# Local attention and retention: ScalarE normalises the shifted tile and squares the retention, the mask comes from row halves, VectorE rotates the last queries, the first release stands first

## The reference

```python
qk = jnp.einsum('bhsd,bhtd->bhst', qr, kr) * mask
denom = jnp.clip(jnp.abs(jax.lax.stop_gradient(qk).sum(-1, keepdims=True)), 1.0, None)
qk = qk / denom
out = jnp.einsum('bhst,bhtd->bhsd', qk, vr).transpose(0, 2, 1, 3)
mu = out.mean(-1, keepdims=True)
var = ((out - mu) ** 2).mean(-1, keepdims=True)
out = (out - mu) / jnp.sqrt(var + 1e-05)
out = jax.nn.silu(g) * out.reshape(B, S, H * head_dim)
return out @ Wo + bo
```

```python
h = shift_token(x)              # second half of the features comes from the token before
q, k, v = jnp.split(h @ wqkv, 3, axis=-1)
q = l2norm(q) * qs
k = l2norm(k) * ksc
q, k = rotary_xpos(q, k)
o = local_attention(q, k, v)    # mask = (i < j) | (i > j + WINDOW) | (j == -1)
x = x + o @ wo
h = shift_token(x)
mu = h.mean(-1, keepdims=True)
var = h.var(-1, keepdims=True)
h = (h - mu) / jnp.sqrt(var + 1e-05) * lg + lb
a, g = jnp.split(h @ w1 + b1, 2, axis=-1)
x = x + (a * jax.nn.gelu(g, approximate=False)) @ w2 + b2
```

## Time and profile before

| | us |
|---|---|
| median of three runs | 1041.69 |
| lowest, highest | 1039.55, 1044.32 |
| the profiled execution, its own time | 1053.3 |
| its span, first to last instruction | 1051.6 |
| TensorE busy | 879.2 (84%) |
| VectorE busy | 662.8 (63%) |
| ScalarE busy | 491.4 (47%) |
| GpSimd busy | 477.9 (45%) |

### The profile page before, as it was taken

The page is one execution under the profiler, slowest core; times in us unless marked ns, Lnnn a source line. Parts: engine busy times, 40 slices in busy tenths (PEclk is TensorE's granted clock), DMA queues, the critical chain, the costliest instruction groups (busy, mean ns, idle before and its releaser), DMA issues.

```text
span 1051.6 us, 19025 instructions
## 1 busy us (share of the span) xinstructions
PE 879.2 (84%) x6808; PEld 540.4 (51%) x6808; DVE 662.8 (63%) x1690; ACT 491.4 (47%) x1010; POOL 477.9 (45%) x501
## 2 busy tenths in 40 slices
PE   5876998889875788899987669988998587888998
PEld 2553676457643344444545536764676344444445
DVE  3897795569678655430168887946795776653302
ACT  2213775367634555542141147744775344655321
POOL 2666883188532422310056678823885324222101
PEclk9999999999996889899989999999999866998999
DMA  9100010011000000000000010100110000000000
GB/s 356 57 1 22 21 28 6 11 26 33 7 1 1 1 2 1 2 1 21 11 13 2 2 32 17 27 2 21 27 28 1 1 1 1 2 1 1 1 20 21
DMA packets 11636, 21.67 MB, mean 21 GB/s; under 512 B 1424, under 2 KB 6928, under 8 KB 11024
## 3 DMA queue, kind: packets, MB, share of 16 engines
q1 hardware_dynamic: 11248, 18.60, 6.0%
q10 hardware_dynamic: 288, 1.78, 0.4%
HBM read 11.87 MB, written 1.05 MB: 12 GB/s over the span
## 4 chain that ended last, share of the span: by engine, by line
PE 53%; DVE 28%; POOL 8%; issue 5%; ACT 4%; DMA 1%; SPq 0%; POOLq 0%; DVEq 0%; ACTq 0%
PE bank L831 11%; PE bank L384 9%; DVE arena L1212 4%; PE bank L742 4%; PE bank L639 3%; PE bank L821 3%; DVE arena L1060 3%; PE bank L709 2%; DVE arena L895 2%; PE bank L728 2%; POOL arena L1722 2%; POOL arena L1730 2%; DVE arena L953 2%; DVE arena L1071 2%; PE bank L414 2%
## 5 line engine op out<-in xcount | busy, mean ns | idle before, releaser
L384 PE MATMUL bank<-consts_sb,arena 128*128 128x128 f32 x1040 | 166.8, 304 | 98.7 <-DVE arena L903 24.3
L384 PEld LDWEIGHTS bank<-consts_sb,arena 128*128 128x128 f32 x1040 | 129.7, 155 | 165.8 <-issue 79.9
L1356 ACT ACTIVATE arena<-bank 128x512 f32<-128x512 f32 (+2 forms) x300 | 147.5, 556 | 143.2 <-PE bank L384 84.8
L1642 POOL TENSOR_TENSOR rstd<-vareps,neghalf 128x1 f32<-128x1 f32 x96 | 53.0, 553 | 250.2 <-DVE vareps L890 248.8
L1212 DVE TENSOR_REDUCE arena<-bank 128x2 f32<-128x1024 f32 (+3 forms) x128 | 98.0, 819 | 47.7 <-PE bank L696 47.0
L1722 POOL TENSOR_TENSOR arena<-arena,neghalf 128x16 f32<-128x16 f32 x32 | 93.1, 2908 | 64.5 <-DVE arena L1062 64.5
L1787 POOL TENSOR_SCALAR_AFFINE_SELECT arena<-arena 128x256 f32<-128x256 f32 x128 | 51.2, 413 | 141.7 <-ACT arena L1554 139.0
L831 PE MATMUL bank<-arena,weights 128*128 128x512 f32 x256 | 111.9, 594 | 1.6 <-ACT arena L1610 1.6
L503 PE MATMUL bank<-weights,x_features 128*128 128x512 f32 x192 | 98.8, 629 | 15.1 <-DVE arena L1075 9.2
L1554 ACT ACTIVATE arena<-bank 128x1024 f32<-128x1024 f32 (+1 forms) x96 | 81.6, 881 | 29.0 <-PE bank L728 28.6
L1474 ACT ACTIVATE arena<-bank,arena 128x128 f32<-128x128 f32 x256 | 69.7, 384 | 50.9 <-DVE arena L1103 50.9
(11 more groups left out here) (172 smaller groups left out, 1643.7 us busy)
## 6 DMA issues: line engine op xcount, KB each, us to landing
arena<-arena SPq DMA_DIRECT2D x56, 130.0 KB, 2.3
weights<-wts_dram SPq DMA_DIRECT2D x1, 2824.0 KB, 19.1
weights<-wts_dram SPq DMA_DIRECT2D x1, 1817.0 KB, 13.1
weights<-wts_dram SPq DMA_DIRECT2D x1, 1561.0 KB, 9.2
arena<-x_dram SPq DMA_DIRECT2D x6, 256.0 KB, 3.2
consts_sb<-consts_dram ACTq DMA_DIRECT2D x1, 1226.5 KB, 7.4
out_dram<-x_inner SPq DMA_DIRECT2D x16, 64.0 KB, 1.5
consts_sb<-consts_dram SPq DMA_DIRECT2D x1, 768.0 KB, 4.5
```

What stands on the lines that cost most here:

```text
L384: mm = pe.transpose(bank[:, i * P:(i + 1) * P], src, ident)
L1356: return act.activation(dst, src, ACT.Copy)
```

## The change

1. `shifted_normed` moves from VectorE to ScalarE: two activations (Identity, with the root as scale and minus mean times root as bias). VectorE keeps one instruction of 128x1, `shifted_mean`, that makes this bias and raises `nm_ready`. ScalarE does its two between the copies of the transposed weights of tile s-2 and the exponentials of tile s-1; its loop now runs to step 12, and the third GELU moves from behind the loop into step 11.
2. The mask of every tile but the first of a sequence comes from 64 rows: a bf16 matrix `twin_bf` (1 where the row and the column agree modulo 64) against the mask's rows 0 to 63 for one bank and rows 64 to 127 for the other. GpSimd makes it in `tables` with two sums of 128x64.
3. In the last tile of a layer VectorE adds and scales the query half (two instructions of 128x512, at the end of its step 7), and GpSimd only the key half.
4. In retention ScalarE takes the square (behind its copy of the same step), and VectorE does `gated` of the tile before between `on1` and the sum of squares.
5. SyncE raises `go` for the first pass as its first instruction.

```diff
+        twin_bf = sb("twin_bf", [P, P], BF16)
@@ TensorE, window_layer
                         for c in range(2):
                             bank = take(pe, ("S", n, c), [(P_ready, 2 * n + c + 1)], bank=BANK2["S"][c])
-                            pe.matmul(bank[:].rearrange("p (h j) -> p h j", h=4), ident_bf[:],
-                                      band_bf[:, first:first + 1, :].to_broadcast([P, 4, P]),
-                                      start=True, stop=False, skip_group_check=True)
+                            scores = bank[:].rearrange("p (h j) -> p h j", h=4)
+                            if first == 0:
+                                pe.matmul(scores, ident_bf[:], band_bf[:, 0:1, :].to_broadcast([P, 4, P]),
+                                          start=True, stop=False, skip_group_check=True)
+                            else:
+                                rows = slice(64 * c, 64 * c + 64)
+                                pe.matmul(scores, twin_bf[rows, :], band_bf[rows, 1:2, :].to_broadcast([64, 4, P]),
+                                          start=True, stop=False, skip_group_check=True)
@@ VectorE, retention: normalise and the loop
-                    dve.wait_ge(on_ready, g + 1)
-                    link(dve.tensor_tensor(sq1[:], on1[:, g % 2], on1[:, g % 2], ALU.mult))
+                    if g:
+                        gated(g - 1)
+                    dve.wait_ge(sq1_ready, g + 1)
                     link(dve.tensor_reduce(a1["ss"], sq1[:], AX, ALU.add))
...
                     normalise(s - 1)
-                    if s >= 2:
-                        gated(s - 2)
@@ VectorE, window_layer
-                def shifted_normed(g):
-                    norm_apply(first + g, hn2[:, g % 2, 0:64], xi[:, g, 0:64])
-                    norm_apply(first + g, hn2[:, g % 2, 64:P], hn2[:, g % 2, 64:P]).then_inc(hn_ready, 1)
+                def shifted_mean(g):
+                    k = first + g
+                    dve.wait_ge(rstd_ready, k + 1)
+                    dve.tensor_scalar(a2["nm"][:, g % 2:g % 2 + 1], meanvar[:, k % 4, 0:1], rstd[:, k % 4:k % 4 + 1], -1.0,
+                                      ALU.mult, ALU.mult).then_inc(nm_ready, 1)
+
+                def queries_rotated(n):
+                    half = slice(0, 512)
+                    dve.wait_ge(swapped_ready, 2 * n + 1)
+                    dve.tensor_tensor(straight2[:, half], straight2[:, half], swapped2[:, half], ALU.add)\
+                        .then_inc(q_rotated, 1)
+                    dve.wait_ge(q_rotated, n + 1)
+                    dve.wait_ge(rn_ready, n + 1)
+                    dve.wait_ge(pe_qT, n - 1)
+                    dve.tensor_tensor(qk2[:, n % 2, half].rearrange("p (h d) -> p h d", d=D2),
+                                      straight2[:, half].rearrange("p (h d) -> p h d", d=D2),
+                                      rn2[:, n % 2, 0:H2].unsqueeze(2).to_broadcast([P, H2, D2]), ALU.mult)\
+                        .then_inc(q_ready, 1)
...
+                    if s == LAST_TILE:
+                        queries_rotated(G * l + s)
@@ ScalarE, retention
                     evac(oE1[:, g % 2, :], held(("oT1", g))[:]).then_inc(oE_ready, 1)
+                    act.wait_ge(on_ready, g + 1)
+                    if g:
+                        act.wait_ge(gvar_ready, g)
+                    act.activation(sq1[:], on1[:, g % 2], ACT.Square).then_inc(sq1_ready, 1)
@@ ScalarE, window_layer
+                def shifted_normed(g):
+                    n, k = G * l + g, LN2 + G * l + g
+                    act.wait_ge(nm_ready, n + 1)
+                    for half, src in ((slice(0, 64), xi[:, g, 0:64]), (slice(64, P), hn2[:, g % 2, 64:P])):
+                        ins = act.activation(hn2[:, g % 2, half], src, ACT.Identity, bias=a2["nm"][:, g % 2:g % 2 + 1],
+                                             scale=rstd[:, k % 4:k % 4 + 1])
+                    ins.then_inc(hn_ready, 1)
...
+                    if s >= 5:
+                        shifted_normed(s - 5)
...
-                    if s > G:
+                    if G < s < G + 4:
                         gelu(l, 0, s - G - 1)
@@ GpSimd, window_layer
+                                if g == LAST_TILE and half == 0:
+                                    continue
@@ SyncE
+            sp.sem_inc(go)
             sp.dma_start(C[:, 0:CONST_CUTS[1]], consts[:, 0:CONST_CUTS[1]]).then_inc(consts_loaded[0], 16)
...
-            sp.sem_inc(go)
```

12 lines of the change are left out of this document (8 added, 4 removed).

## The result

The changed kernel takes 1015.62 us, the median of 4 runs (1012.38 to 1020.96), beside 1043.01 us for the kernel before (4 runs, 1039.55 to 1054.54). The ratio is 0.971, with a 95% interval of 0.967 to 0.976. The forecast was 1010 us, with a range of 1000 to 1026. Run once more, on the chip of the last experiments, the same kernel gave 0.977 (0.972 to 0.982).

A forecast was written before the change was run, and what follows sets the result against it. TensorE and VectorE were both taken as full in the local attention's steady steps. Layers 20.8, retention 8.0 and start 3.0 sum to 31.8 us off 1053.3, so 1021.5, scaled to 1010 us; range 1000 to 1026.

The forecast's parts named there:

- Steady steps and the mask: Local attention: TensorE gives back 0.6 us a layer in short waits for the queries, and the mask 1.3 us.
- VectorE's step falls from 9.2 to 7.7 us, so TensorE becomes the only bound: Local attention's steady steps: VectorE loses 1.65 us and gets one 128x1 instruction, taken as 0.2 us.
- 8.7 to 8.9 us: Local attention: expected length of steady steps, with TensorE busy throughout and VectorE idle over 1 us.
- tail: Steps following a layer's last tile: two instructions before the copy that frees a bank become one; 0.3 us a layer.
- TensorE gives nothing: Rival, chance 0.12: in steady steps the masks don't overlap or TensorE's waits were none; 7.6 us lost, 1017.5 us.
- The last tile: Last tile of each layer: queries ready earlier, 1.8 us (bounds 0.9 and 2.4), and TensorE's clock staying up, 1.2 us.
- Retention: Retention: 4.0 us a pass, 8.0 in all, including 0.8 a pass for slow stretches; bounds 2.0 and 6.5 a pass.
- The product's place: Retention: the gated product comes 1.02 us earlier, counted as 1.0 us in two steps where TensorE's chain is the bound.
- Four steps at 0.3: Retention: in four steps VectorE gets back only the square, 0.42 us, less 0.1 for the way to ScalarE and back.
- The start: Kernel start: TensorE begins 3.5 us earlier, bounded by VectorE's idle 3.12 us; 3.0 us taken, bounds 2.0 and 3.5.
- The slower rival: Rival, chance 0.03: ScalarE becomes the bound if its pair is stretched, deciding from 2.05 us a pair; 1058 us.
- The scale: Whole kernel: 1021.5 us in the profiled execution, 1.1% above the runs' median, scaled by 1041.69 / 1053.3 to 1010 us.

The follow-up runs named there:

- experiment 10: On the changed kernel, VectorE copies the shifted tile first, then sums squares, with statistics last and GpSimd's root behind the rotation; 0.987 of the kernel before.

## Why the prediction was right, and where it was not

The total was right: 30.5 us by the stages, 31.8 forecast. The sum is closer than its terms, and that is luck: the layers gave 5.5 us less than forecast, retention 2.2 and the start 2.0 more, and much of what came in their place is TensorE's clock.

- **Steady steps and the mask: wrong.** The step that failed is "VectorE's step falls from 9.2 to 7.7 us, so TensorE becomes the only bound". A loop over GpSimd of 18.4 us in two steps bounds them, just as long as TensorE's and VectorE's fill were. I read the busy times of single engines and took 100% for the bound; the queries' short waits inside the transposes were the visible end of the loop. VectorE was a bound of 9.19 us in before, where the chain of waits runs along it through the steady steps; taking the pair off it laid bare the loop, 9.13, and breaking the loop (experiment 10) laid bare TensorE, 9.01. So even without the loop my 8.7 to 8.9 us were out of reach on the average, for the mask is worth 0.12 us a tile and not 0.22. Steady steps, mask and tail were to give 2.2 us a layer; 0.3 came, 7.6 us less over four layers. (The layers gave 15.3 of 20.8 us, since the first gained some 1.6 by the clock in its third step, which the second run didn't repeat.) The outcome is that of my rival "TensorE gives nothing", held at 0.12, but neither of its two reasons: the masks do overlap, and the waits were real. Its 1017.5 us missed only since other terms were larger.
- **The last tile: right.** 1.8 by the wait and 1.2 by the clock were forecast, 3.0. Measured are 2.9 to 3.15: 1.07 for the queries on VectorE, 0.4 for its earlier arrival, and 1.4 to 1.7 for the clock. The first term was too large by 0.3 (the sum on VectorE began while GpSimd's product ran, 0.88 us for 0.69), the second too small. The clock's share is no certain gain: in the kernel of the start release alone the clock was up without this edit, and with all queries on VectorE it fell in three of four layers in spite of it. In both runs of after it stayed up in all four.
- **Retention: 10.2 for 8.0, inside its bounds.** The product's place is worth 1.0 us in one step, not two; in the other TensorE was late only through its clock (7.06 us with it up, 8.0 to 8.1 with it down). Four steps at 0.3 were five that sum up to 1.2, and the last step, which was to stay, gave another 0.3. The clock is worth 2.7 a pass (1.7 and 1.0 in the two steps) and not 0.8. The hand-over to ScalarE costs what I said, but the reason that it pays was not in the prediction: it takes the square out of GpSimd's product.
- **The start: 5.0 for 3.0.** I let VectorE's wait bound it; TensorE has no gap until 29 us, so its whole lead of 3.6 us counts. The other 1.3 are its first projections, which ran faster here than in most kernels (4.61 us; 4.21 to 5.67), so only the 3.6 are the edit's for certain.
- **The slower rival** was wrong on the point and the price. Its 2.05 us a pair isn't worked out from a row; in after the pair and the wait behind it are 0.8 + 0.85 us, so the wait is gone from about 1.65 us on. At 2.0 us a pair it is gone and the steady steps stay; what it costs, it costs behind the last tile.
- **The scale.** I scaled the sum to the median of the runs with the 1.1% of one execution, and so kept nearly all of the 31.8 us as a gain on 1041.69. By the ratios the gain is 30 us in the first set of runs and 24 in the second, so 1010 us was low by 5.6 for one set and by about 8 for the other (0.977 x 1041.69 = 1018).

## What to carry to other kernels

Two engines at 100% of a step may be full by chance: follow the chain of waits through two whole steps, and add up the loop that returns to the same instruction one tile later, before pricing what a relieved engine gives. When several edits meet in one step, measure them in pairs, since a gain may need both. And price what is moved at the edges of the pipeline too, where nothing covers it.

## What the runs showed of the hardware

An elementwise instruction of VectorE with its inputs in SBUF that starts while GpSimd's sum, product or memset runs is held, and ends shortly behind GpSimd's end: 128x64 takes 1.30 us (0.31 alone) and ends 0.04 us behind it, 128x256 0.95 (0.42) and 0.29, 128x512 1.08 (0.69) and 0.54, and 128x16 beside a memset 1.55 (0.17) and 0.03. Not everything is held. The 128x1 forms keep their 0.15 to 0.22 us, the sum over 128x1024 takes 1.21 us in before beside GpSimd's 128x512 and without it, and a 128x256 product that starts in a memset at 12.85 in after takes 0.42.

The order of the start matters, but not always as the profile's starts have it. The square of before, started 0.04 us ahead of GpSimd's product, took 0.42 us; a 128x128 instruction (L895, at 117.58 in before), started 0.07 us ahead of one, took 1.20 and not 0.34. ScalarE's pair of 128x64 shows 0.42 to 0.49 us in every kernel.

The same idle time of TensorE (1.69 us) was followed by a granted clock of 0.50 in one kernel and 1.00 in another, and in one kernel by both in different layers, so the clock's price is to be stated as a range.
